# First attention of a four-block model: the eight row maxima of a batch in consecutive slots, and four steps moved with them

## The chip, the cores and the metric

The kernel runs on one core of one Trainium2 chip. The metric is the device time of one execution in microseconds, the median of several. Engine names are those of the profile: PE is the matrix engine and PEld its weight load, DVE the vector engine, ACT the scalar engine, POOL the general engine, SP the queue that issues transfers.

## The reference, cut to what matters

Four blocks follow one another on `x` of 16 batches of 256 tokens and 128 channels: a mixed attention, a feed-forward layer, a second pair of attentions and a mixture of experts. Only the first block is touched:

```
x = x + attention0(layernorm(x), ctx)
    q, cq, k, v = z @ Wq + bq, z @ Wcq + bcq, z @ Wk + bk, z @ Wv + bv     # 16 heads of 8
    ck, cv      = ctx @ Wck + bck, ctx @ Wcv + bcv                         # 64 context tokens a batch
    y  = softmax(causal(q k^T / sqrt 8)) v  +  softmax(cq ck^T / sqrt 8) cv
    out = y @ Wp + bp
```

The softmax subtracts the maximum of each row. The kernel finds the maxima of a batch with scores of its own, puts them, negated, into spare rows of the queries, and computes the scores a second time, transposed, with the maximum already taken off.

## The kernel before, in words

`l0_attention` works through 16 batches in a software pipeline. A batch has U = 10 slots; slot number s = 10 n + u is slot u of batch n, and each engine has its own program, written out slot by slot by `tensor_slot`, `vector_slot`, `scalar_slot` and `gpsimd_slot`. Each engine runs its own list strictly in order, and semaphores tie the four together. Slot u of batch n holds the second scores of one unit of that batch (u 0 to 7 self attention, u 8 and 9 context), the exponential of them on ACT, and, in between, steps of other batches. The table `SLOT` says how many slots from slot 0 of its own batch a step stands: `nm` at -3 is slot 7 of the batch before. In what follows u0 to u9 are the ten slots of the steady state, and a step is named by the u in which it falls.

The steps: `z` transposes the normalised tokens; `qk0` and `qk1` are the projections of q, cq and k of both token tiles; `v`, `ck`, `cv` those of the values and of the context; `q0`, `q1`, `k`, `kc` transpose the queries and keys; `nm` transposes the maxima; `e0`, `e1` and `e2` transpose the unnormalised outputs (self attention of both token tiles, and context), DVE divides them by their sums, and after `e2` adds the context part to the self part (`y_summed`); `e3` transposes the sum, ACT copies it out, and `e4` multiplies it with `Wp`. All of them go through a ring of two PSUM banks (6 and 7): a step on PE waits until the step two before it in the ring has been drained by DVE or ACT. Within one slot the order is that of `SLOT`: z, q0, q1, v, k, qk0, kc, ck, cv, qk1, nm, e0 to e4.

The maxima of a batch are eight steps m0 to m7: four `late` (rows 128 to 255 of the tokens), two `early`, two `cross` (context). Each is a group of matmuls into PSUM banks 2 and 3 (`tensor_max`) and a reduction over both banks by DVE (`vector_max`). Both banks are filled and read by every step, so the matmuls of m(k+1) wait for the reduction of m(k). The `late` and `early` steps come early in their slot on each engine, right behind the scores, the `cross` steps last. Before the change m0 to m4 stand in u8, u9, u0, u1 and u2, none in u3, m5 in u4, m6 in u5 and m7 in u6.

When m7 is done, `nm` puts the maxima on 32 rows, ACT copies them to `a_nmT`, SP issues four small transfers of them into the spare rows of `a_QT`, and `tensor_scores` of slot u0 waits for all four (`nm_placed`). `gpsimd_context` copies the context of a batch into `a_ctx`, for which `ck` waits. POOL also masks the exponentials (`gpsimd_select`), splits the keys (`gpsimd_stack`), raises the variances to a power (`gpsimd_rstd`) and, in u5 of batches 1 to 11, splits one piece of the feed-forward weights (`ffn.gpsimd_split`).

Slots from -40 to -1 are the lead-in: the first batches are projected and the maxima of batch 0 made before there are any scores. The slots from 164 on run inside the first slots of `l0_ffn`: slot 164 + i stands at the end of its slot i on each engine.

Of the kernel before, what the change touches and what calls it, by code (L numbers as in the profile page):

```python
# [15 lines left out]
X = mybir.AxisListType.X  # L16

P = 128
B, T, C, CC, TC = 16, 256, 128, 64, 64
# [222 lines left out]
def l0_attention(pr, mem, ffn, meanwhile):  # L242
# [4 lines left out]
    nc, io, psum = pr.nc, pr.io, pr.psum  # L247
    D, G, W = 8, 4, 32
    NM = 3 * D
    SCALE = 1.0 / float(np.sqrt(D))  # L250
    U, M, NV = 10, 8, 5
# [37 lines left out]
    nm = pr.sb("a_nm", [P, 2, 4, 2, G], F16, mem)  # L289
# [9 lines left out]
    for i in range(3):  # L299
        nc.vector.memset(V[i][:, :, :, D:D + 1], 1.0)  # L300
        for a in range(2):
# [11 lines left out]
    max_full, max_done, nm_placed = pr.sem("a_max_full"), pr.sem("a_max"), pr.sem("a_nm_placed")  # L313
# [5 lines left out]


    SLOT = {"z": -28, "q0": -20, "q1": -16, "v": -14, "k": -15, "qk0": -24, "kc": -13, "ck": -23, "cv": -13,
            "qk1": -22, "nm": -3, "e0": 12, "e1": 13, "e2": 13, "e3": 18, "e4": 20}
    MAXIMA = {m: m - (12 if m < 5 else 11) for m in range(M)}
    FIRST, LAST = -4, B + 1

    def batches(n, u, slots):

        pairs = [(part, *divmod(U * n + u - slot, U)) for part, slot in slots.items()]
        return [(part, batch) for part, batch, rest in pairs if rest == 0 and 0 <= batch < B]

    def projections(n, u):
        return batches(n, u, SLOT)
# [15 lines left out]

    first_maxima = lambda n, u: [(m, batch) for m, batch in batches(n, u, MAXIMA) if maxima[m][0] != "cross"]
    last_maxima = lambda n, u: [(m, batch) for m, batch in batches(n, u, MAXIMA) if maxima[m][0] == "cross"]  # L350

    def score_bank(n, u):

        return 2 * (u % 2) if n == B - 1 else 0


    def tensor_drained(use):
        engine, count = ring.drain[use]
        if engine == "a":
            nc.tensor.wait_ge(pro_a, count)  # L360
        else:
            nc.tensor.wait_ge(pro_v, count)
# [107 lines left out]
    def tensor_max(n, m):  # L470
        q, k, kc = QT[n % 3], KT[n % 3], KcT[n % 3]
        kind, e, pair = maxima[m]
        if m == 0:
            tensor_drained(("k", n))
        if kind == "cross":
            tensor_drained(("kc", n))
        if n or m:
            nc.tensor.wait_ge(max_done, M * n + m)
        if kind == "late":
            for x in range(2):  # L480
                for i in range(2):
                    r, g = rows(2 * e + i), 2 * pair + x
                    nc.tensor.matmul(psum[:, 2 + i, x * T:x * T + T], q[r, 0, g, P:T], k[r, g, :], start=(x == 0),
                                     stop=False, skip_group_check=True)
            for i in range(2):
                diagonal = psum[:, 2 + i, :].rearrange("p (a h k) -> p a h k", a=2, h=2)[:, :, 1, :]
                inst = nc.tensor.matmul(diagonal, pr.identb[:, :], pr.hide_later[:, 0:2, :], start=False, stop=True,  # L487
                                        skip_group_check=True)
        elif kind == "early":
            for g in range(G):  # L490
                for i in range(2):
                    r = rows(2 * e + i)
                    nc.tensor.matmul(psum[:, 2 + i, g * P:g * P + P], q[r, 0, g, 0:P], k[r, g, 0:P], start=(g == 0),
                                     stop=False, skip_group_check=True)
            for i in range(2):
                inst = nc.tensor.matmul(psum[:, 2 + i, :], pr.identb[:, :],
                                        pr.hide_later[:, :, :].rearrange("p a k -> p (a k)"), start=False, stop=True,
                                        skip_group_check=True)
        else:
            for t in range(2):  # L500
                for g in range(G):
                    for i in range(2):
                        r, to = rows(2 * e + i), (t * G + g) * TC
                        inst = nc.tensor.matmul(psum[:, 2 + i, to:to + TC], q[r, 1, g, t * P:t * P + P], kc[r, g, :],
                                                start=(t == 0 and g == 0), stop=True, skip_group_check=True)
        inst.then_inc(max_full, 1)

# [45 lines left out]
    def vector_normed(n, k):  # L553
        src = pr.x[:, 2 * n:2 * n + 2, :]
        if k == 0:
            nc.vector.wait_ge(pr.x_in[n // 2], 16)
            ln.vector_stats(n, src)
        else:
            if n >= 2:
                nc.vector.wait_ge(pro_full, ring.full(("z", n - 2)))  # L560
            ln.vector_normalise(n, z[n % 2], src).then_inc(z_ready, 1)

    def vector_max(n, m):
        kind, e, pair = maxima[m]
        pe = slice(2 * e, 2 * e + 2)
        nc.vector.wait_ge(max_full, M * n + m + 1)
        if m == 0 and n:
            nc.vector.wait_ge(pro_full, ring.full(("nm", n - 1)))
        if kind == "late":
            out, groups = nm[:, 1, pe, 0, 2 * pair:2 * pair + 2], 2  # L570
        elif kind == "early":
            out, groups = nm[:, 0, pe, 0, :], 4
        else:
            for t in range(2):
                inst = nc.vector.tensor_reduce(
                    nm[:, t, pe, 1, :], psum[:, 2:4, t * T:t * T + T].rearrange("p i (a b) -> p i a b", a=G), X,
                    ALU.max, negate=True)
            inst.then_inc(max_done, 1)
            return
        nc.vector.tensor_reduce(out, psum[:, 2:4, :].rearrange("p i (a b) -> p i a b", a=groups), X, ALU.max,  # L580
                                negate=True).then_inc(max_done, 1)

    def vector_projection(use):
# [53 lines left out]
    def vector_slot(s):  # L637
        n, u = divmod(s, U)
        for m, batch in first_maxima(n, u):
            vector_max(batch, m)  # L640
        for use in projections(n, u):
            if DRAIN[use[0]] == "v":
                vector_projection(use)
        for m, batch in last_maxima(n, u):
            vector_max(batch, m)
        for k, batch in batches(n, u, {0: -36, 1: -29}):
            vector_normed(batch, k)
        if n == B - 1 and u in (2, 5):
            ffn.vector_normed(0, u // 5)
        if n == B and u in (2, 5):  # L650
            ffn.vector_normed(1, u // 5)
# [67 lines left out]
    def gpsimd_context(n):  # L719
        if n >= 2:  # L720
            nc.gpsimd.wait_ge(pro_full, ring.full(("cv", n - 2)))
        nc.gpsimd.wait_ge(pr.ctxT_in, 16)
        nc.gpsimd.tensor_copy(ctx2[n % 2][:, :].rearrange("c (a t) -> c a t", a=2),
                              pr.ctxT[:, n:n + 1, :].to_broadcast([CC, 2, TC])).then_inc(ctx_ready, 1)
# [20 lines left out]
    def gpsimd_select(n, u):  # L745
        unit = U * n + u
        nc.gpsimd.wait_ge(exp_done, unit + 1)
        diagonal = prob[unit % 5][:, :, :].rearrange("p i (b k) -> p (i b) k", b=2)[:, :, 0:P]
        nc.gpsimd.affine_select(out=diagonal, in_=diagonal, compare_op=ALU.is_ge, fill=0.0, base=0,  # L749
                                pattern=[[0, 4], [1, P]], channel_multiplier=-1).then_inc(sel_done, 1)  # L750

    def gpsimd_slot(s):
        n, u = divmod(s, U)
        if u < 8 and 0 <= n < B:
            gpsimd_select(n, u)
        for _, batch in batches(n, u, {0: -34}):
            ln.gpsimd_rstd(batch)
        for _, batch in batches(n, u, {0: -24}):
            gpsimd_context(batch)
        for t, batch in batches(n, u, {0: -21, 1: -18, 2: -17}):  # L760
            gpsimd_stack(batch, t)
        if u == 5 and 1 <= n <= len(ffn.pieces):
            ffn.gpsimd_split(n - 1)
        if n >= B - 1 and u == 3 and n <= B:
            ffn.ln.gpsimd_rstd(n - B + 1)
# [548 lines left out]
class SelfAttention:  # L1314
# [9 lines left out]
    U, G, D = 8, 4, 32  # L1324
# [447 lines left out]
class CrossAttention:  # L1772
# [9 lines left out]
    U, G, D = 8, 4, 32  # L1782
    SLOT = {"z": -11, "k": -8, "q0": -7, "q1": -6, "v": -4, "nm": -1, "o": 14}
    SCORES, VALUES, MAXIMA = {0: 0, 1: 2}, {0: 3, 1: 5}, -4
    FIRST, LAST = -23, 8 * (B - 1) + 17
# [203 lines left out]
    def tensor_slot(self, s):  # L1989
        for e, n in self.parts(s, self.SCORES):  # L1990
            self.tensor_scores(n, e)
        for _, n in self.parts(s, {0: self.MAXIMA}):
            self.tensor_max(n)
# [73 lines left out]
    def vector_slot(self, s):  # L2067
        for _, n in self.parts(s, {0: self.MAXIMA}):
            self.vector_max(n)
# [667 lines left out]
```

## Time and profile before

| | us |
|---|---|
| median of 3 runs (1500.03 to 1508.36) | 1507.75 |
| the profiled execution's own time | 1501.43 |
| its span | 1499.7 |
| lead-in to the first scores | 0 to 48.6 |
| batches 0 to 15 of the first attention | 48.6 to about 386 |
| everything behind it | to 1499.7 |

The views used below are the page itself, the busy time of each engine in stretches of the span, the chain of work that ended last, who waited for whom, and the timeline of one engine. A timeline row has the start in us, the duration, engine and line, the operation and its operands, the count of instructions merged into it, and in square brackets the idle time before it and what ended that.

### The profile page before, as it was taken

The numbers are of one execution on the slowest core, as the hardware profiler recorded it, in microseconds if no ns is written. First come the engines' busy times: TensorE is split into PE (matmuls) and PEld (weight loads), VectorE is DVE, ScalarE is ACT, GpSimd is POOL, SyncE is SP. The second block draws the span as 40 slices with busy tenths as digits, with TensorE's granted clock in tenths as the row PEclk, the third lists the DMA queues.
The fourth block names the chain that finished last, engine by engine and source line by source line (L and its number), as shares of the span: only waits on it lengthen the run. The fifth ranks groups of instructions, "written<-read, shape, count | busy, mean of one in ns | idle before, by whom it ended". The sixth has DMA issues, their size and how long they took to land.

```text
span 1499.7 us, 42738 instructions
## 1 busy us (share of the span) xinstructions
PE 1351.0 (90%) x17848; PEld 856.9 (57%) x17848; DVE 977.7 (65%) x2238; ACT 845.7 (56%) x1309; POOL 649.5 (43%) x1118
## 2 busy tenths in 40 slices
PE   5899999997899998899999999997989999998695
PEld 2455555554344444455666666664766777677484
DVE  4777777775454544577788787745667887675232
ACT  2577777775465555657666666653456666432231
POOL 3355545543200001335666566343337775354155
PEclk9999999998999999999999999998999999998798
DMA  6000000000600000000000000012001111032351
GB/s 214 3 3 2 3 2 3 3 3 2 161 1 1 1 1 0 1 2 17 30 17 31 30 17 31 22 39 57 1 16 45 56 48 45 29 99 73 122 158 43
DMA packets 54514, 53.76 MB, mean 36 GB/s; under 512 B 9273, under 2 KB 48574, under 8 KB 54067
## 3 DMA queue, kind: packets, MB, share of 16 engines
q1 hardware_dynamic: 50482, 44.24, 9.7%
q0 software_dynamic: 2816, 6.11, 1.2%
q8 instruction: 142, 2.33, 0.7%
q10 hardware_dynamic: 1024, 0.69, 0.2%
q14 instruction: 50, 0.40, 0.1%
HBM read 20.34 MB, written 14.49 MB: 23 GB/s over the span
## 4 chain that ended last, share of the span: by engine, by line
PE 65%; DVE 12%; ACT 6%; issue 5%; POOL 5%; DMA 3%; SPq 3%; POOLq 0%; DVEq 0%; ACTq 0%
PE psum L1499 6%; PE psum L911 4%; PE psum L913 3%; PE psum L912 3%; PE psum L1182 3%; PE psum L1527 3%; DVE a_nm L580 3%; PE psum L1148 3%; PE psum L2496 2%; PE psum L2512 2%; PE psum L1976 2%; SPq L772 2%; DMA a_QT<-a_nmT 2%; DVE b_nm L1583 2%; PE psum L1985 2%
## 5 line engine op out<-in xcount | busy, mean ns | idle before, releaser
L1583 DVE TENSOR_REDUCE b_nm<-psum 128x4 f16<-128x1024 f32 x128 | 157.5, 1230 | 70.0 <-PE psum L1504 69.0
L697 ACT ACTIVATE a_prob<-psum 128x768 f32<-128x768 f32 (+1 forms) x160 | 136.1, 853 | 62.5 <-PE psum L460 60.6
L580 DVE TENSOR_REDUCE a_nm<-psum 128x4 f16<-128x1024 f32 (+1 forms) x96 | 117.4, 1223 | 50.2 <-PE psum L487 35.8
L749 POOL TENSOR_SCALAR_AFFINE_SELECT a_prob<-a_prob 128x512 f32<-128x512 f32 x128 | 81.7, 639 | 129.5 <-ACT a_prob L697 129.3
L170 POOL TENSOR_TENSOR f_ln_rstd<-f_ln_tmp,pow_half 128x4 f32<-128x4 f32 x24 | 25.3, 1056 | 204.6 <-DVE f_ln_tmp L159 204.6
L1040 ACT ACTIVATE xo_sb<-psum,f_w_h_s 128x512 f32<-128x512 f32 x64 | 44.0, 688 | 87.0 <-PE psum L913 87.0
L1499 PE MATMUL psum<-b_QTh,b_KTh 32*128 32x256 f16 x512 | 71.2, 272 | 11.7 <-DVE b_nm L1583 8.5
L1504 PE MATMUL psum<-b_KTh,b_QTh 32*128 32x256 f16 x512 | 70.7, 273 | 1.5 <-DVE b_nm L1583 1.5
L1499 PE MATMUL psum<-b_QTh,b_KTl 32*128 32x256 f16 x512 | 70.2, 268 | 0.0
L1499 PE MATMUL psum<-b_QTl,b_KTh 32*128 32x256 f16 x512 | 70.2, 267 | 0.0
L1504 PE MATMUL psum<-b_KTl,b_QTh 32*128 32x256 f16 x512 | 69.5, 268 | 0.0
L1504 PE MATMUL psum<-b_KTh,b_QTl 32*128 32x256 f16 x512 | 69.5, 268 | 0.0
L1705 POOL TENSOR_SCALAR_AFFINE_SELECT b_late<-f_hT1l 128x256 f32<-128x256 f32 x64 | 28.2, 463 | 88.7 <-ACT f_hT1l L1668 88.7
L2606 POOL DMA_INDIRECT out_dram<-m_ys,m_number x40 | 39.7, 991 | 55.2 <-DVE m_ys L2547 45.1
L980 DVE TENSOR_TENSOR f_hlastl<-xo_sb,f_hlasth 128x512 f16<-128x512 f32 x32 | 22.2, 692 | 53.0 <-ACT f_hlasth L1041 53.0
L980 DVE TENSOR_TENSOR f_hT1l<-xo_sb,f_hT1h 128x512 f16<-128x512 f32 x32 | 22.5, 702 | 51.6 <-ACT f_hT1h L1041 51.6
L911 PE MATMUL psum<-f_hT0h,f_h_wh 128*128 128x512 f16 x128 | 50.1, 392 | 5.9 <-DVE f_hT0l L974 5.9
L1499 PEld LDWEIGHTS psum<-b_QTh,b_KTh 32*128 32x128 f16 x512 | 25.4, 92 | 45.3 <-issue 27.8
L913 PE MATMUL psum<-f_hT0h,f_h_wl 128*128 128x512 f16 x128 | 50.0, 391 | 0.0
L912 PE MATMUL psum<-f_hT0l,f_h_wh 128*128 128x512 f16 x128 | 49.8, 389 | 0.0
L1511 PE MATMUL psum<-b_nmT,b_group_row 32*128 32x256 f16 x512 | 49.1, 268 | 0.0
L1668 ACT ACTIVATE f_hT0h<-psum 128x1024 f32<-128x1024 f32 x32 | 32.7, 1023 | 28.2 <-PE psum L1511 28.2
(448 smaller groups left out, 4637.8 us busy)
## 6 DMA issues: line engine op xcount, KB each, us to landing
f_h_wh<-b_rden SPq DMA_DIRECT2D x64, 128.0 KB, 2.1
f_h_wh<-c_rden SPq DMA_DIRECT2D x64, 128.0 KB, 2.1
expert_in<-empty SPq DMA_DIRECT2D x8, 662.5 KB, 11.0
m_xt<-expert_in SPq DMA_DIRECT2D x8, 662.5 KB
m_w<-in_L_ffn_w_dram SPq DMA_DIRECT2D x16, 256.0 KB
x_sb<-in_x_dram SPq DMA_DIRECT2D x8, 256.0 KB, 4.6
f_w_h_w<-in_L_ffn_h_w_dram SPq DMA_DIRECT2D x2, 1024.0 KB, 7.5
out_dram<-m_send SPq DMA_DIRECT2D x8, 256.0 KB, 2.5
```

The source lines that it names most:

```text
L580: nc.vector.tensor_reduce(out, psum[:, 2:4, :].rearrange("p i (a b) -> p i a b", a=groups), X, ALU.max, negate=True).then_inc(max_done, 1)
L697: nc.scalar.activation(prob[unit % 5][:, :, 0:width], psum[:, first:first + 2, 0:width], ACT.Exp, scale=SCALE).then_inc(exp_done, 1)
L749: nc.gpsimd.affine_select(out=diagonal, in_=diagonal, compare_op=ALU.is_ge, fill=0.0, base=0, pattern=[[0, 4], [1, P]], channel_multiplier ...
L911: nc.tensor.matmul(bank, wh[:, k, m * P:m * P + P], xh[:, k, :], start=(k == 0), stop=False)
L912: nc.tensor.matmul(bank, wh[:, k, m * P:m * P + P], xl[:, k, :], start=False, stop=False)
L913: inst = nc.tensor.matmul(bank, wl[:, k, m * P:m * P + P], xh[:, k, :], start=False, stop=(k == K4 - 1))
L1148: nc.tensor.matmul(psum[:, u % 3, :], li2[:, slot * P:slot * P + P], zT[n % 2][:, :], start=True, stop=True).then_inc(full, 1)
L1182: inst = nc.tensor.matmul(bank[:, to], hT[n % 2][:, k, to], li3[:, k, :], start=(t == 0 and k == 0), stop=True, skip_group_check=True)
L1499: t.matmul(psum[:, first_bank + i, to], key[r, g, own], q[r, g, :], start=(k + first + second == 0), stop=False, skip_group_check=True)
L1504: inst = t.matmul(psum[:, 2 + i, to], q[r, g, own], key[r, g, :], start=(k + first + second == 0), stop=(first == 1), skip_group_check=True)
L1511: inst = t.matmul(psum[:, first_bank + i, k * T:k * T + T], self.group_row[r, g, :], self.nmT[n % 2][r, :], start=False, stop=True, skip_g ...
L1583: v.tensor_reduce(self.nm[:, :, :].rearrange("p t (j r) -> p j t r", r=32)[:, 2 * e:2 * e + 2, :, g], self.pr.psum[:, 2:4, :].rearrange("p ...
```

## The change

Six edits, all in `l0_attention`:

1. m5, m6 and m7 come one slot sooner (u3, u4 and u5), so that the eight maxima stand in u8, u9, u0 to u5.
2. `nm` comes one slot sooner, in u6 behind v and qk0, in place of u7 behind kc, ck and cv. ACT's copy and SP's four transfers follow it.
3. `gpsimd_context` stands in u0, six slots sooner, in place of u6. The statistics of the layer norm go from u4 to u6, and their power on POOL from u6 to u8; the normalisation stays in u1.
4. `e2`, with its division and the sum on DVE, goes from u3 to u7 behind kc, ck and cv; `e3` goes from u8 to u9. `e4` stays in u0.
5. In batch 0 alone the odd maxima use banks 0 and 1 (free, since there are no scores yet) and the even ones 2 and 3; the matmuls of m(k) then wait for the reduction of m(k-2).
6. For batch 15, `e2` falls in slot 167 and `e3` in 169: inside slots 3 and 5 of `l0_ffn`. Before they fell in 163 and 168, the first of them still in the attention's own loop.

```diff
     SLOT = {"z": -28, "q0": -20, "q1": -16, "v": -14, "k": -15, "qk0": -24, "kc": -13, "ck": -23, "cv": -13,
-            "qk1": -22, "nm": -3, "e0": 12, "e1": 13, "e2": 13, "e3": 18, "e4": 20}
-    MAXIMA = {m: m - (12 if m < 5 else 11) for m in range(M)}
+            "qk1": -22, "nm": -4, "e0": 12, "e1": 13, "e2": 17, "e3": 19, "e4": 20}
+    MAXIMA = {m: m - 12 for m in range(M)}
...
+    def max_bank(n, m):
+
+        return 0 if n == 0 and m % 2 else 2
...
-        if n or m:
+        if n:
             nc.tensor.wait_ge(max_done, M * n + m)
+        elif m > 1:
+            nc.tensor.wait_ge(max_done, m - 1)
+        first = max_bank(n, m)
...
-                    nc.tensor.matmul(psum[:, 2 + i, x * T:x * T + T], q[r, 0, g, P:T], k[r, g, :], start=(x == 0),
+                    nc.tensor.matmul(psum[:, first + i, x * T:x * T + T], q[r, 0, g, P:T], k[r, g, :], start=(x == 0),
...
-        pe = slice(2 * e, 2 * e + 2)
+        pe, banks = slice(2 * e, 2 * e + 2), slice(max_bank(n, m), max_bank(n, m) + 2)
...
-        nc.vector.tensor_reduce(out, psum[:, 2:4, :].rearrange("p i (a b) -> p i a b", a=groups), X, ALU.max,
+        nc.vector.tensor_reduce(out, psum[:, banks, :].rearrange("p i (a b) -> p i a b", a=groups), X, ALU.max,
...
-        for k, batch in batches(n, u, {0: -36, 1: -29}):
+        for k, batch in batches(n, u, {0: -34, 1: -29}):
             vector_normed(batch, k)
...
-        for _, batch in batches(n, u, {0: -34}):
+        for _, batch in batches(n, u, {0: -32}):
             ln.gpsimd_rstd(batch)
-        for _, batch in batches(n, u, {0: -24}):
+        for _, batch in batches(n, u, {0: -30}):
             gpsimd_context(batch)
```

## Rows read from the trace of the kernel before

**Rows 1.** The page, part 1: busy time of each engine

```profile
PE 1351.0 (90%) x17848; PEld 856.9 (57%) x17848; DVE 977.7 (65%) x2238; ACT 845.7 (56%) x1309; POOL 649.5 (43%) x1118
```

**Rows 2.** Stretches: length, busy time by engine, TensorE clock, DMA share, GB/s

```profile
110.34:130.91 20.57, 18.84 (x266) 11.03 (x266) 16.18 (x34) 15.00 (x22) 11.13 (x20) 1.00 0.01 2
297.92:317.72 19.80, 18.87 (x267) 11.04 (x268) 15.40 (x29) 15.00 (x22) 8.81 (x17) 1.00 0.02 4
...
252.00:256.00 4.00, 4.00 (x37) 1.42 (x39) 2.59 (x3) 2.91 (x5) 1.05 (x2) 0.50 0.03 8
```

**Rows 3.** Chain of work that ended last, one batch: start, us, what

```profile
108.52 1.77 DMA a_QT<-a_nmT
...
111.15 1.22 DVE a_nm L580
```

**Rows 4.** Timeline of PE, one batch from u0 to u8

```profile
110.39 0.28 PE L483 MATMUL psum<-a_KT,a_QT 32*128 32x256 f16 x2
...
114.46 0.40 PE L493 MATMUL psum<-a_KT,a_QT 32*128 32x128 f16 x8
...
115.98 0.28 PE L456 MATMUL psum<-a_QT,a_KT 32*128 32x256 f16 x2
...
117.53 0.60 PE L429 MATMUL psum<-ident,a_ysT 128*128 128x128 f32 x4
...
125.51 0.68 PE L382 MATMUL psum<-a_wctx,a_ctx 64*128 64x128 f32 x4 [0.84 <-POOL a_ctx L723]
126.34 0.28 PE L409 MATMUL psum<-ident,a_nm 128*32 128x128 f16 x2 [0.15 <-DVE a_kcf L597]
126.55 0.41 PE L466 MATMUL psum<-a_QT,a_KcT 32*64 32x256 f16 x8
```

**Rows 5.** Timeline of DVE, the same batch

```profile
113.18 1.22 DVE L580 TENSOR_REDUCE a_nm<-psum 128x4 f16<-128x1024 f32 x1
...
115.43 1.23 DVE L580 TENSOR_REDUCE a_nm<-psum 128x8 f16<-128x1024 f32 x1 [0.52 <-PE psum L496]
...
118.23 0.35 DVE L624 RECIPROCAL a_denc<-psum 128x32 f32<-128x32 f32 x1
...
119.41 1.22 DVE L580 TENSOR_REDUCE a_nm<-psum 128x8 f16<-128x1024 f32 x1
...
127.65 1.23 DVE L580 TENSOR_REDUCE a_nm<-psum 128x4 f16<-128x1024 f32 x1 [0.83 <-PE psum L487]
```

**Rows 6.** Timeline of PE, a batch without a piece of weights on POOL

```profile
311.96 0.29 PE L404 MATMUL psum<-ident,a_kctok 64*128 64x64 f16 x4
...
312.72 0.49 PE L382 MATMUL psum<-a_wctx,a_ctx 64*128 64x128 f32 x2 [0.17 <-ACT a_KcT L668]
313.13 0.29 PE L409 MATMUL psum<-ident,a_nm 128*32 128x128 f16 x2
```

**Rows 7.** Timeline of PE, the lead-in

```profile
28.64 0.61 PE L483 MATMUL psum<-a_KT,a_QT 32*128 32x256 f16 x4 [1.32 <-DVE a_nm L580]
...
43.87 0.29 PE L409 MATMUL psum<-ident,a_nm 128*32 128x128 f16 x2 [0.52 <-DVE a_kcf L597]
...
48.65 0.28 PE L456 MATMUL psum<-a_QT,a_KT 32*128 32x256 f16 x2 [1.81 <-DMA a_QT<-a_nmT]
```

**Rows 8.** Timeline of PE: m4 of batch 15, then its first slot

```profile
341.33 0.40 PE L493 MATMUL psum<-a_KT,a_QT 32*128 32x128 f16 x8 [0.54 <-DVE a_nm L580]
...
355.86 0.40 PE L456 MATMUL psum<-a_QT,a_KT 32*128 32x256 f16 x2 [0.52 <-DMA a_QT<-a_nmT]
```

**Rows 9.** Timeline of PE and ACT, the end of the attention inside the feed-forward

```profile
385.75 1.19 PE L438 MATMUL psum<-a_wp,a_yT 128*128 128x128 f32 x4 [4.54 <-ACT a_yT L675]
...
386.21 0.63 ACT L1033 ACTIVATE f_hT0h<-xo_sb 128x512 f16<-128x512 f32 x1 [0.60 <-DVE xo_sb L969]
```

**Rows 10.** Chain of work that ended last: a reduction in u0 of two batches

```profile
235.08 1.23 DVE a_nm L580
...
278.15 1.23 DVE a_nm L580
```

More of the change, by code:

```diff
@@ L482, in tensor_max @@
                     r, g = rows(2 * e + i), 2 * pair + x
-                    nc.tensor.matmul(psum[:, 2 + i, x * T:x * T + T], q[r, 0, g, P:T], k[r, g, :], start=(x == 0),
+                    nc.tensor.matmul(psum[:, first + i, x * T:x * T + T], q[r, 0, g, P:T], k[r, g, :], start=(x == 0),
                                      stop=False, skip_group_check=True)
             for i in range(2):
-                diagonal = psum[:, 2 + i, :].rearrange("p (a h k) -> p a h k", a=2, h=2)[:, :, 1, :]
+                diagonal = psum[:, first + i, :].rearrange("p (a h k) -> p a h k", a=2, h=2)[:, :, 1, :]
                 inst = nc.tensor.matmul(diagonal, pr.identb[:, :], pr.hide_later[:, 0:2, :], start=False, stop=True,
@@ L492, in tensor_max @@
                     r = rows(2 * e + i)
-                    nc.tensor.matmul(psum[:, 2 + i, g * P:g * P + P], q[r, 0, g, 0:P], k[r, g, 0:P], start=(g == 0),
+                    nc.tensor.matmul(psum[:, first + i, g * P:g * P + P], q[r, 0, g, 0:P], k[r, g, 0:P], start=(g == 0),
                                      stop=False, skip_group_check=True)
             for i in range(2):
-                inst = nc.tensor.matmul(psum[:, 2 + i, :], pr.identb[:, :],
+                inst = nc.tensor.matmul(psum[:, first + i, :], pr.identb[:, :],
                                         pr.hide_later[:, :, :].rearrange("p a k -> p (a k)"), start=False, stop=True,
@@ L503, in tensor_max @@
                         r, to = rows(2 * e + i), (t * G + g) * TC
-                        inst = nc.tensor.matmul(psum[:, 2 + i, to:to + TC], q[r, 1, g, t * P:t * P + P], kc[r, g, :],
+                        inst = nc.tensor.matmul(psum[:, first + i, to:to + TC], q[r, 1, g, t * P:t * P + P], kc[r, g, :],
                                                 start=(t == 0 and g == 0), stop=True, skip_group_check=True)
@@ L575, in vector_max @@
                 inst = nc.vector.tensor_reduce(
-                    nm[:, t, pe, 1, :], psum[:, 2:4, t * T:t * T + T].rearrange("p i (a b) -> p i a b", a=G), X,
+                    nm[:, t, pe, 1, :], psum[:, banks, t * T:t * T + T].rearrange("p i (a b) -> p i a b", a=G), X,
                     ALU.max, negate=True)
```

## The prediction

> **What bounds the kernel now.** I read the page first: PE is busy 90% and DVE 65% [rows 1], but these are averages over four blocks, and only the first attention, 338 of 1500 us, is touched. So I cut that stage by batch. A batch of the steady state takes 20.57 us, of which PE is busy 18.84 and DVE 16.18 [rows 2]: PE is nearest to the bound and still idles 1.7 us. Batches 1 to 11 of this kind carry a piece of weights on POOL; the next batch takes 19.80 us [rows 2].
>
> The idle time of PE in a batch is of three kinds. First, ck stands 0.84 us because POOL's copy of the context is late, and nm another 0.15 behind DVE's drain of ck [rows 4]. In the batch without a piece of weights that wait is gone; only cv waits 0.17 us for ACT's copy of kc [rows 6]. Second, u0 waits for the transfer of the maxima; it lands at 110.29 (108.52 + 1.77, rows 3), and m2's matmuls start at 110.39 [rows 4]. Third, the maxima wait for one another. A reduction takes 1.22 us, 0.05 later PE may refill the banks, and a late step is ready for DVE 0.76 later (m2: PE at 110.39, DVE at 111.15, rows 3 and 4). So late steps follow one another at 2.03 us: 111.15, 113.18 [rows 3, 5]. The early m4 needs 0.97 on PE (114.46, rows 4; 115.43, rows 5), so its distance is 2.25.
>
> The reader should see that two of these bind at once in u0: m1's reduction ends 0.05 before 110.39 too (one step of 2.03 before m2's start of reduction, plus its 1.22: 111.15 - 2.03 + 1.22 = 110.34). Taking away the transfer's wait frees only the two scores matmuls ahead of m2, which overlap m2 anyway.
>
> **The change part by part.** I walk one batch of the changed kernel from m4's matmuls at 114.46 [rows 4], with u8 to u2 as before, since their maxima already go hand over hand.
>
> *m5 in u3.* m4's reduction ends at 115.43 + 1.23 = 116.66 [rows 5]; m5 starts at 116.71. PE has done u3's scores by 116.25 (115.98 + 0.27) and stands 0.46 us. This wait is new; behind it in PE's order are the values and e1, and ACT gets its next scores later. In u4 before, m5 found its banks free. PE then does m5 0.76, the values 0.79, e1 0.49, u4's scores 0.27 and q1 0.54 (distances between starts on PE's timeline): m6 starts at 119.56, past m5's reduction (116.71 + 0.97 + 1.23 = 118.91). PE sets the pace again from here.
>
> *m6, m7, nm.* m6 0.28, u5's scores 0.27 with 0.14 of waiting for ACT, the values 0.79, k 0.55: m7 at 121.59. Then m7 0.28, u6's scores 0.27, v 0.65, qk0 0.85, 0.07 for DVE's drain of v (queued behind m7's reduction), nm 0.22: u7 at 123.93. nm starts at 123.71 in place of 126.34 [rows 4], so its transfers land 2.6 us sooner, long before u0. On SP nothing else is queued.
>
> *kc, ck, cv, e2 in u7.* Scores 0.27, values 0.79, kc; the context has been there since u0. But cv still waits for ACT's copy of kc: it starts 0.76 behind kc (311.96 to 312.72, rows 6) and takes 0.41. Before, this wait lay under the late context. Then e2, 0.53 (it started at 117.53, rows 4, and u4's scores at 118.06), moved here from u3. Sum: u8 at 123.93 + 1.06 + 0.76 + 0.41 + 0.53 = 126.69, against 126.55 [rows 4]. What the context's wait gave (0.99), the new wait in u3 (0.46), the uncovered copy of kc and the two cross steps, less well overlapped, have taken back.
>
> *The sum on DVE.* e2's matmuls now end just ahead of u8. They are done 0.60 behind their start at 126.16, and DVE needs 1.18 from the first reciprocal until m's reduction may start (118.23 to 119.41, rows 5): 126.16 + 0.60 + 0.05 + 1.18 = 127.99. m0's matmuls would be ready at 127.79. So m0's reduction starts at 127.99 against 127.65 before [rows 5], and everything to the next m4 is the chain of reductions, which hands the delay on: +0.34, say +0.3 us for each of the 11 batches with a piece, +3.3.
>
> The batch without a piece was shorter by 20.57 - 19.80 = 0.77 us [rows 2]; with the changed order the piece makes no difference any more, so there the change costs 0.34 + 0.77 = +1.1 for each of two batches: +2.2.
>
> Bounds for a batch: from -1.5 (both named waits go, 0.48 + 0.99, and nothing comes in their place) to +1.1 (what the walk gives with no late context to win back). I take +0.3, as each term is a distance in this trace.
>
> *Statistics, power and context moved.* DVE's statistics (0.9 us) go behind qk0's drain in u6, where PE's next need of DVE is kc 1 us later; POOL has no mask to make in u8. Cost nothing under these covers; without them at most their own 0.9 us, and then only against the copy of ck.
>
> *e3 in u9, e4 in u0.* ACT's queue in u9 is an exponential, a copy and a cast, then e3's copy; e4 wants it 1.3 us into u0. ACT had 0.40 us idle there. Nothing, at most 0.4.
>
> *Batch 0.* In the lead-in PE stands 1.32 us before m2 [rows 7], as much before m4, 0.47 before m3 and 0.89 before m5. With two bank pairs these go, and m5 to m7 come sooner by a slot. I walked it with the low clock's durations: m2 27.1, m3 29.0, m4 29.9, m5 32.6 (z waits for the normalisation that DVE queues behind m3), m6 34.8, m7 36.4, nm 39.5 in place of 43.87 [rows 7]. Batch 1's m0 then starts about 41.3 instead of 44.09, and m2 in u0, at the end of the chain of two reductions, 3.2 us sooner than with the first scores at 48.65 [rows 7]. So nm's 4.4 us don't arrive whole, because batch 1's own maxima bind next. -3.2, between 0 and -5.
>
> *Batch 15.* In batch 14 no projections are left and the maxima bind alone. From m4 at 341.33 [rows 8] the chain gives m5 343.58, m6 345.9, m7 347.7, nm 349.6, and 4.6 us later (nm at 313.13, rows 6, to the next u0 at 317.72, rows 2) u0 at 354.3 in place of 355.86 [rows 8]: -1.5. In its tail the feed-forward's PE stands 4.54 us for ACT's copy of e3 [rows 9]. One slot later that copy is queued behind the cast at 386.21 as well [rows 9] (before, it started at 385.23), some 1.6 us; e2's DVE work out of the way of the first product gives back some 0.7. +0.9.
>
> **Sum:** -3.2 + 3.3 + 2.2 - 1.5 + 0.9 = +1.7 us. Against the profiled execution's own 1501.43 that is 1503; against the median of 1507.75 it would be 1509. The shown runs lie at 1500 and at 1508, so neither is a firm base; I say 1507.
>
> **The clock.** Over a whole batch the granted clock is 1.00 in spite of the small waits [rows 2]. The Trainium skill (TensorE: Matmul & The Clock Gate, section on psum-queue depth-cycling) tells of a kernel whose PE idles briefly between groups while it cycles through PSUM banks and whose clock goes up and down because of it. No steady batch but one does so here; the rival below is what it would mean.
>
> **The rivals.**
>
> *The waits simply go.* If m5 didn't stand in u3 and DVE weren't late for m0, each batch would lose its 1.47 us: -16.2 for eleven, -1.3 for two, with the ends (-3.8) -21 us: 1486. For it: PE is the busiest engine, and both waits are on the chain. Against it: the chain of reductions, tied with the transfer in u0. Chance 0.10.
>
> *Clock dips.* The slower side. Once, at 252 to 256, the clock fell to half, 0.50 [rows 2], some 3 us behind the wait for the context in a thin stretch of PE's work. The two batches around it took 278.15 - 235.08 = 43.07 us [rows 10] in place of 41.14: 1.9 us a dip. The change spreads PE's idling over u9 to u3, where m1 to m5 all stand. If that made each of 14 batches dip once, it would cost 27 us more: 1534. It decides from eight dips on (15 us). The profile's clock of 1.00 speaks against, and the stretch after kc gets denser. Chance 0.05.
>
> *The slot edit doesn't overlap anything in batch 0* (PE was the limit there): +3.2 on the sum, 1510, inside my case. Chance 0.15. The forecast, a loss of a few tenths in each batch balanced by the lead-in, has the other 0.70.
>
> **How the numbers follow.** A measurement of this kernel tells about 1%, 15 us, from no change. Forecast and third rival lie within it, save for 0.01 below and 0.02 above, where the walk errs by 1 us a batch. Faster over 1% 0.11, within 0.82, slower 0.07. The range takes the per-batch term from -0.9 to +0.9 less the ends, and the 8 us between the runs: 1491 to 1517.
>
> **What would show it.** Right: m5's matmuls start in u3 behind an idle of about 0.46 put down to DVE; ck no longer waits for POOL, cv waits for ACT; m0's reduction starts right behind DVE's sum; u0 has no wait for the transfer, but the batch still takes 20.6 to 21.1 us; the first scores start near 45; e4 of batch 15 stands longer. Wrong: a batch of 19 to 20 us, or several batches with a clock of about 0.8. The walk would be wrong if PE's steps overlap otherwise than in their present order, since each tenth in a batch is 1.4 us in all.

## The result and the profile after

The changed kernel takes 1514.84 us (median of 20 runs, 1505.62 to 1520.43) against 1505.09 for the kernel before (median of 20). The ratio is 1.0056, 95% interval 1.0041 to 1.0071: 8.4 us slower (the two medians are 9.75 apart). The forecast was 1507 with a loss of 1.7 us inside the noise; the loss is clear of it.

A batch first. The stretches below run from u8's scores to the next u8's; columns are length, busy time of PE, PEld, DVE, ACT and POOL, the granted clock, the DMA share and GB/s. After the change:

```profile
44.68:64.44 19.76, 17.34 (x189) 8.34 (x188) 11.20 (x19) 10.31 (x15) 7.80 (x15) 0.68 0.01 2
106.65:127.88 21.23, 19.89 (x267) 10.96 (x266) 16.35 (x36) 14.89 (x22) 11.13 (x21) 1.00 0.01 2
```

The second line answers to the 20.57 us of [rows 2]: 0.66 us more in ten of the batches 1 to 11 (batch 1 took 20.98), at the same clock of 1.00. The first is batch 0 from its first scores to u8, and its clock is 0.68.

The timeline of PE after the change, from u8 to the next u8:

```profile
107.54 0.81 PE L382 MATMUL psum<-a_wcat,a_zT 128*128 128x384 f32 x2
...
109.26 0.39 PE L490 MATMUL psum<-a_KT,a_QT 32*128 32x256 f16 x4 [0.57 <-DVE a_nm L587]
...
115.37 0.40 PE L500 MATMUL psum<-a_KT,a_QT 32*128 32x128 f16 x8
...
117.62 0.40 PE L500 MATMUL psum<-a_KT,a_QT 32*128 32x128 f16 x8 [0.40 <-DVE a_nm L587]
117.95 0.60 PE L503 MATMUL psum<-hide_later,identb 128*128 128x512 bf16 x2
118.49 0.64 PE L527 MATMUL psum<-a_prob,a_V 128*32 128x256 f32 x8
...
119.28 0.66 PE L426 MATMUL psum<-ident,a_ysT 128*128 128x128 f32 x4
119.86 0.28 PE L460 MATMUL psum<-a_QT,a_KT 32*128 32x256 f16 x2
...
124.84 0.28 PE L413 MATMUL psum<-ident,a_nm 128*32 128x128 f16 x2
...
126.88 0.48 PE L386 MATMUL psum<-a_wctx,a_ctx 64*128 64x128 f32 x2 [0.17 <-ACT a_KcT L675]
127.30 0.66 PE L433 MATMUL psum<-ident,a_ysT 128*128 128x128 f32 x4
127.88 0.41 PE L470 MATMUL psum<-a_QT,a_KcT 32*64 32x256 f16 x8
```

Read it against [rows 4]. The wait of ck for POOL is gone and that of u0 for the transfer too. In their place m5 (117.62) stands 0.40 us for m4's reduction, cv 0.17 for ACT's copy of kc, and m1 (109.26) 0.57 for m0's reduction. The last comes of DVE, whose timeline has the sum of e2 right ahead of m0's reduction:

```profile
106.80 0.36 DVE L631 RECIPROCAL a_denc<-psum 128x32 f32<-128x32 f32 x1
107.19 0.42 DVE L633 TENSOR_TENSOR a_yc<-psum,a_denc 128x256 f32<-128x256 f32 x1
107.65 0.42 DVE L636 TENSOR_TENSOR a_y<-a_y,a_yc 128x256 f32<-128x256 f32 x1
107.99 1.22 DVE L587 TENSOR_REDUCE a_nm<-psum 128x4 f16<-128x1024 f32 x1
```

u8's scores started at 106.65, so m0's reduction comes 1.34 us behind them; before it was 127.65 - 126.55 = 1.10 [rows 4, 5]. So both halves of the batch are longer: from m4's matmuls to u8 it is 12.51 us (115.37 to 127.88) against 12.09 (114.46 to 126.55, rows 4), and from u8 to the next m4 0.24 more, which is DVE's sum.

Where the 8 us lie by the two traces, from one u8 to the next: u8 of batch 0 is 0.4 us sooner (64.44 against 64.84); batches 1 to 11 take 21.23 us each against 20.57, in all 4.6 us more, since the trace of before had three longer batches (22.50, 20.91, 20.74) in them; batches 12 to 15 take 1.45, 1.55, 0.98 and 0.10 us more. u8 of batch 15 starts at 375.21 against 366.98: +8.2 us. From there to the first matmul of the feed-forward's second layer it is 22.29 us against 21.04, and at the first reduction of the second attention the changed kernel is 8.0 us late (634.5 against 626.5). The two profiled executions differ by more, 1513.0 against 1499.7 us of span: the other 5.3 us arise behind 990 us, in code that the change leaves alone, and the execution profiled before was 3.7 us faster than its kernel's median. What follows therefore counts the traces up to the end of the first attention only.

### The profile page after: what moved, and what is told of

Read it like the earlier page. It is cut to its first block, busy times and chain, and to the rows that moved or that the text cites. A ratio compares the mean times of both kernels' runs of the same rounds, so it can differ in the third digit from the quotient of the medians.

```text
span 1513.0 us, 42738 instructions
## 1 busy us (share of the span) xinstructions
PE 1368.8 (90%) x17848; PEld 858.4 (57%) x17848; DVE 979.1 (65%) x2238; ACT 844.7 (56%) x1309; POOL 651.2 (43%) x1118
## 3 DMA queue, kind: packets, MB, share of 16 engines
HBM read 20.34 MB, written 14.49 MB: 23 GB/s over the span
## 4 chain that ended last, share of the span: by engine, by line
PE 70%; DVE 15%; ACT 6%; issue 4%; POOL 2%; DMA 1%; SPq 1%; POOLq 0%; DVEq 0%; ACTq 0%
PE psum L1506 6%; DVE a_nm L587 5%; PE psum L918 4%; PE psum L919 3%; PE psum L1189 3%; PE psum L920 3%; PE psum L1534 3%; PE psum L1155 3%; PE psum L2503 2%; PE psum L527 2%; PE psum L2519 2%; PE psum L1983 2%; DVE b_nm L1590 2%; PE psum L1992 2%; PE psum L1930 2%
## 5 line engine op out<-in xcount | busy, mean ns | idle before, releaser
L582 DVE TENSOR_REDUCE a_nm<-psum 128x8 f16<-128x512 f32 x64 | 41.2, 686 | 20.8 <-PE psum L511 20.8
```

## The experiments

Twelve kernels ran. In the diffs, only the lines that differ from the kernel named are shown. "A batch" is the distance from u8 to u8 that most of the batches 1 to 11 of one profile share to 0.02 us. Single batches are longer in several kernels, and each kernel has one profile only.

### Each edit alone, on the kernel before

**The third edit** (context, statistics, power):

```diff
-        for k, batch in batches(n, u, {0: -36, 1: -29}):
+        for k, batch in batches(n, u, {0: -34, 1: -29}):
...
-        for _, batch in batches(n, u, {0: -34}):
+        for _, batch in batches(n, u, {0: -32}):
             ln.gpsimd_rstd(batch)
-        for _, batch in batches(n, u, {0: -24}):
+        for _, batch in batches(n, u, {0: -30}):
             gpsimd_context(batch)
```

> The kernel before with the third edit alone: the context copied in u0, statistics in u6, power in u8. Theory (each batch is a chain of PE and DVE steps, and the late context is a real link of it): batches 1 to 11 go from 20.57 us to the 19.80 us of the batch that had no piece of weights, ck no longer waits for POOL, the kernel is 8 us faster (ratio 0.995). Rival (the context's wait is covered by the transfer of the maxima in u0, as both reach u0 together): a batch stays at 20.5 us and the time is unchanged.

Measured: ratio 1.0004 (0.9977 to 1.0032), a batch 20.40 us (two of 20.76 and 20.74). Neither theory: the context's wait is gone, but nm stands. What the batches give, the ends of its trace take back: u8 of batch 0 comes at 68.73 against 64.84, and batches 14 and 15 take 4.2 us more; why wasn't tried.

```profile
129.05 0.49 PE L382 MATMUL psum<-a_wctx,a_ctx 64*128 64x128 f32 x2 [0.17 <-ACT a_KcT L668]
130.08 0.28 PE L409 MATMUL psum<-ident,a_nm 128*32 128x128 f16 x2 [0.54 <-DVE a_kcf L597]
```

Its DVE shows why; the statistics moved to u6 run between m7's reduction and the drain of ck, for which nm waits:

```profile
127.67 1.28 DVE L575 TENSOR_REDUCE a_nm<-psum 128x8 f16<-128x512 f32 x2
128.87 0.47 DVE L150 BATCH_NORM_STATS2 aln_stat<-x_sb 128x6 f32<-128x128 f32 x2
129.38 0.25 DVE L154 BATCH_NORM_AGGREGATE aln_mv<-aln_stat 128x2 f32<-128x6 f32 x2
129.66 0.17 DVE L159 TENSOR_SCALAR aln_tmp<-aln_mv 128x2 f32<-128x2 f32 x1
129.74 0.28 DVE L597 TENSOR_TENSOR a_kcf<-psum,a_bctx 64x128 f32<-64x128 f32 x1
```

**The fourth edit** (sums): `"e2": 13, "e3": 18` becomes `"e2": 17, "e3": 19`.

> The kernel before with the fourth edit alone: e2 and its sum in u7, e3 in u9. Theory (DVE's 1.2 us of division and sum now stand ahead of m0's reduction, which heads the chain m0 to m4): m0's reduction starts right behind the sum and a batch takes 20.9 to 21.1 us, the kernel is 4 to 7 us slower. Rival (the sums are harmless, the loss is all in the maxima): a batch of 20.6 us, within 1 us of before.

Measured: ratio 1.0114 (1.0076 to 1.0153), 17 us where the theory had 4 to 7, a batch 21.23 us, and five of the eleven 23.1 to 23.4. So this edit alone costs as much per batch as the whole change, and PE's clock falls in batches besides:

```profile
104.73:125.97 21.24, 19.32 (x267) 11.01 (x267) 16.19 (x34) 14.98 (x22) 11.09 (x20) 1.00 0.01 2
170.51:193.92 23.41, 22.02 (x267) 11.64 (x266) 16.42 (x34) 15.09 (x22) 11.08 (x20) 0.85 0.01 3
```

Two batches of one kernel with the same instructions; the second has a clock of 0.85 and is 2.2 us longer. This is the mechanism of my slower rival, in a kernel that the rival didn't name; the changed kernel's profile has no such batch between 1 and 11.

**The first two edits** (maxima and nm): `"nm": -3` becomes `-4`, `m - (12 if m < 5 else 11)` becomes `m - 12`.

> The kernel before with the first two edits alone: m5, m6, m7 and nm one slot sooner. Theory (m5's matmuls now stand in u3 behind m4's reduction, and everything on PE behind them is late): an idle of 0.4 us before m5, u0 waits no longer for the transfer, a batch takes 21.0 to 21.3 us, the kernel is 5 to 9 us slower. Rival (the transfer's wait of 0.48 us was a real link): a batch of 20.1 to 20.3 us, 4 us faster.

Measured: ratio 1.0057 (1.0037 to 1.0076), a batch 20.96 us; PE idles 0.40 us before m5, and u0 shows no wait for the transfer. The theory holds (its batch was 0.04 too long), the rival falls: without its wait in u0 a batch is longer, not shorter. These edits also cost time ahead of the steady batches: u8 of batch 0 comes at 69.70 against 64.84.

**The fifth edit** (two bank pairs in batch 0): the lines with `max_bank` of the diff above.

> The kernel before with the fifth edit alone: the odd maxima of batch 0 on banks 0 and 1. Theory (the lead-in gets shorter, but PE's clock stays at half for longer, so that batch 0 gives it back): nm of batch 0 some 3 us sooner, the first scores 2 to 4 us sooner, u8 of batch 0 less than 1 us sooner, the kernel's time the same within 1.5 us. Rival (the lead-in's gain arrives whole, and the other edits ate it): u8 of batch 0 is 3 us sooner and the kernel 3 us faster.

Measured: ratio 0.9969 (0.9948 to 0.9990). The first scores come at 45.12 against 48.65 [rows 7], u8 of batch 0 at 62.93 against 64.84: half of the 3.5 us is given back in batch 0, between theory and rival. The expected "same" falls, if narrowly: the ratio says 1.5 to 7.8 us, 4.7 by its middle, of which the trace shows 1.9 in batch 0 (the profiled execution was the slowest of the twelve, 1508.54 us).

### From the fastest kernel back to the changed one

**The context's copy alone**, statistics and power left where they were:

```diff
-        for _, batch in batches(n, u, {0: -24}):
+        for _, batch in batches(n, u, {0: -30}):
             gpsimd_context(batch)
```

> The kernel before with the context's copy alone moved to u0; statistics and power stay in u4 and u6. Theory (in the run with the whole third edit it was DVE's statistics, now ahead of its drain of ck, that nm waited 0.54 us for, not the context any more): nm waits for nothing but kc's copy, batches 1 to 11 take 19.8 us, the kernel is 7 to 9 us faster (ratio 0.995). Rival (something else reaches u7 just after the context, such as POOL's masks behind the piece of weights): 20.4 us a batch as in that run, 0 to 2 us faster.

Measured: ratio 0.9905 (0.9888 to 0.9923), a batch 19.79 us. On the timeline of PE only u0 (108.58) and cv (123.37) still stand:

```profile
108.58 0.28 PE L456 MATMUL psum<-a_QT,a_KT 32*128 32x256 f16 x2 [0.49 <-DMA a_QT<-a_nmT]
...
123.37 0.48 PE L382 MATMUL psum<-a_wctx,a_ctx 64*128 64x128 f32 x2 [0.17 <-ACT a_KcT L668]
```

Eleven batches at 0.78 us are 8.6 us; the measured 14 us are more. Three of before's batches were longer than 20.57 in its profile and one of this kernel's was longer than 19.79 (20.34), so that u8 of batch 15 comes 11.1 us sooner by the traces (355.86 against 366.98); the rest of the difference isn't found in the first attention.

**The same with two bank pairs in batch 0.**

> The kernel before with the context's copy alone moved, and the two bank pairs in batch 0. Theory (the two parts touch different stretches and add up): 11 to 13 us faster than before (ratio 0.992), u8 of batch 0 some 2 us sooner, then 19.8 us a batch. Rival (with less waiting the clock falls more often, so that the sum does not arrive): under 8 us faster.

Measured: ratio 0.9885 (0.9870 to 0.9900), 1491.57 us, the lowest median, and 17 us where the theory had 11 to 13. The bank pairs' own part, 0.9885 against 0.9905, isn't clear of the noise: the intervals overlap. u8 of batch 0 comes at 60.88 against 64.62 with the context's copy alone: here all 3.8 us of the lead-in arrive. The two stretches from the first scores to u8, with the two bank pairs alone, and with the context's copy too:

```profile
45.12:62.93 17.81, 16.26 (x186) 8.43 (x187) 10.31 (x20) 10.00 (x13) 8.50 (x16) 0.71 0.01 2
```

```profile
44.70:60.88 16.18, 14.26 (x185) 7.76 (x186) 10.26 (x19) 9.89 (x13) 8.52 (x16) 0.79 0.01 3
```

Equal work, clocks of 0.71 and 0.79, 1.6 us apart: by these two, what of the lead-in's gain arrives is a matter of where PE's clock comes back.

**m5 alone into u3**, with the context's copy in u0: `m - (12 if m < 5 else 11)` becomes `m - (12 if m < 6 else 11)`.

> The kernel before with the context's copy in u0 (as in the run that gave 19.79 us a batch), and m5 alone moved from u4 to u3; m6, m7 and nm stay. Theory (m5's matmuls find their banks held by m4's reduction and PE stands with all of u3 and u4 queued behind): an idle of 0.40 us before m5 in each batch, u5 starts 5.8 us behind m4's matmuls in place of 5.1, a batch takes 20.4 to 20.6 us, 8 us more than without this edit. Rival (the wait in u3 is won back in u4, where PE has less to do): 19.8 to 20.0 us.

Measured: ratio 1.0034 (1.0009 to 1.0059), a batch 20.88 us, 1.09 more than without the edit, and more than the theory's 0.7; the kernel is 1.3%, 19 us, slower than without it, where the theory had 8. First PE here, from m4 to u5, then ACT, then PE of the kernel before in u4:

```profile
137.16 0.40 PE L493 MATMUL psum<-a_KT,a_QT 32*128 32x128 f16 x8
...
139.41 0.40 PE L493 MATMUL psum<-a_KT,a_QT 32*128 32x128 f16 x8 [0.39 <-DVE a_nm L580]
...
140.28 0.64 PE L520 MATMUL psum<-a_prob,a_V 128*32 128x256 f32 x8
...
142.09 0.28 PE L456 MATMUL psum<-a_QT,a_KT 32*128 32x256 f16 x2
...
142.40 0.62 PE L393 MATMUL psum<-ident,a_tok 128*128 128x128 f16 x8
143.33 0.28 PE L456 MATMUL psum<-a_QT,a_KT 32*128 32x256 f16 x2 [0.31 <-ACT a_prob L697]
```

```profile
142.47 0.81 ACT L697 ACTIVATE a_prob<-psum 128x768 f32<-128x768 f32 x1 [2.60 <-PE psum L460]
```

```profile
118.06 0.28 PE L456 MATMUL psum<-a_QT,a_KT 32*128 32x256 f16 x2
...
118.24 0.38 PE L493 MATMUL psum<-a_KT,a_QT 32*128 32x128 f16 x8
...
119.00 0.61 PE L393 MATMUL psum<-ident,a_tok 128*128 128x128 f16 x8
```

From m4 to u5 it is 6.17 us here against 5.08 in the kernel before (114.46 to 119.54). By distances between starts the 1.09 has three parts. m5 starts 0.46 us later than PE was free for it (0.39 of it shown as idle). u5's scores (143.33) wait for ACT's exponential of u4, which isn't queued late, since ACT had been idle 2.60 us when u4's scores came; PE, with m5 gone from u4, reaches u5 before it is done, and that costs 0.39. And m5 takes 0.87 us in u3 (139.41 to 140.28), while u4 gets shorter without it by 0.63 only (from the scores to the next transposes 0.94 with it, 0.31 without): in u4 it began 0.18 us behind the scores and ran into them. That is the last 0.24.

**All of m5, m6, m7 and nm**, with the context's copy in u0.

> The kernel before with the context's copy in u0, and m5, m6, m7 and nm one slot sooner. Theory (the first two edits alone make the batch of the run that had all but the sums): 20.8 us a batch in place of 19.79, no wait for the transfer in u0, 12 us more than without them, of which m5 is two thirds. Rival (statistics on DVE in u6 or the two bank pairs had a share in that run's 20.83): 20.4 us or less.

Measured: ratio 1.0080 (1.0050 to 1.0110), a batch 20.96 us. m6, m7 and nm add 0.08 to m5's 1.09. Not two thirds but nearly all of it is m5. The whole kernel is 26 us slower than without these edits, where the theory had 12: eleven batches at 1.17 are 12.9, and u8 of batch 0 comes at 70.74 against 64.62. On the kernel before the same two edits cost 0.39 a batch (20.57 to 20.96), not 1.17: there the wait of ck for the context shrank in exchange, from 0.84 to 0.28 us.

**The sums alone**, with the context's copy in u0: `"e2": 17, "e3": 19`.

> The kernel before with the context's copy in u0, and e2 with its sum in u7, e3 in u9. Theory (0.14 us of PE, as transposes overlap less well there, and 0.24 us of DVE ahead of m0): a batch takes 20.1 to 20.3 us in place of 19.79, 4 to 6 us more than without it. Rival (what made this edit alone cost 0.66 us a batch was the late context): 19.8 to 19.9 us.

Measured: ratio 1.0030 (1.0006 to 1.0053), a batch 20.67 us, 0.88 more, and 19 us in all where the theory had 4 to 6. My 0.4 was too small, for a reason that the profile names:

```profile
126.00 0.66 PE L429 MATMUL psum<-ident,a_ysT 128*128 128x128 f32 x4 [0.47 <-DVE a_Vc L607]
126.59 0.41 PE L466 MATMUL psum<-a_QT,a_KcT 32*64 32x256 f16 x8
...
129.16 0.39 PE L483 MATMUL psum<-a_KT,a_QT 32*128 32x256 f16 x4 [0.53 <-DVE a_nm L580]
```

With nm still in u7, e2 is two behind cv in the ring of banks and waits 0.47 us for DVE to drain cv. In the changed kernel nm is in u6, e2 is two behind ck, and that wait doesn't exist: the two edits are coupled through the ring.

**The changed kernel with the sums moved back**: `"e2": 13, "e3": 18`.

> The changed kernel with e2 and its sum back in u3 and e3 back in u8; maxima, nm, context, statistics and banks stay moved. Theory (e2 in u7 costs 0.58 us of PE behind the context and 0.24 us of DVE ahead of m0): m0's reduction starts 1.1 us behind u8 in place of 1.34, a batch takes 20.7 to 20.9 us in place of 21.23, the kernel is 4 to 6 us faster than the changed one (ratio to before 1.002). Rival (the wait of m5 in u3 is the whole loss, e2's place is neutral): 21.1 to 21.3 us a batch, ratio 1.0055.

Measured: ratio 0.9997 (0.9980 to 1.0014), a batch 20.83 us in place of 21.23. The theory holds in the batch: the sums cost 0.40 us each in the changed kernel. The kernel is 9 us faster than the changed one, where the theory had 4 to 6.

**The changed kernel with DVE's order turned**: division and sum of e2 behind m0's reduction, PE untouched.

```diff
+        for use in batches(n, u, {"e2": 18}):
+            vector_projection(use)
         for use in projections(n, u):
-            if DRAIN[use[0]] == "v":
+            if DRAIN[use[0]] == "v" and use[0] != "e2":
```

> The changed kernel with one edit: DVE does e2's division and sum behind m0's reduction, not ahead of it; PE's order is untouched. Theory (0.24 us of the 0.66 a batch is DVE standing in the way of m0's reduction): m0's reduction starts 1.1 us behind u8, a batch takes 21.0 us in place of 21.23, the kernel is 2 to 4 us faster than the changed one (ratio to before 1.0035). Rival (e3 in u9 now waits for the sum, or qk1's drain comes too late for q0): still 21.2 us or more.

Measured: ratio 1.0078 (1.0061 to 1.0095), a batch 21.73 us, the longest of all (in the whole time only the fourth edit alone is slower). m0's reduction does come 1.10 us behind u8 (107.16, 108.26), but the next one is late:

```profile
108.26 1.23 DVE L587 TENSOR_REDUCE a_nm<-psum 128x4 f16<-128x1024 f32 x1 [0.98 <-PE psum L494]
109.40 0.35 DVE L631 RECIPROCAL a_denc<-psum 128x32 f32<-128x32 f32 x1
109.78 0.42 DVE L633 TENSOR_TENSOR a_yc<-psum,a_denc 128x256 f32<-128x256 f32 x1
110.24 0.42 DVE L636 TENSOR_TENSOR a_y<-a_y,a_yc 128x256 f32<-128x256 f32 x1
110.58 0.55 DVE L599 TENSOR_TENSOR a_qf<-psum,a_bcat 128x384 f32<-128x384 f32 x1
111.05 1.22 DVE L587 TENSOR_REDUCE a_nm<-psum 128x4 f16<-128x1024 f32 x1
```

m0 to m1 is 2.79 us in place of 2.03: between two reductions DVE has 0.8 us to spare while PE refills the banks, and the sum with qk1's drain is 1.65. The rival's number (21.2 or more) came true, but neither of its causes was this one; the step ahead of m0 was the cheaper place for the sum, as PE had work of its own there.

**kc in u6**, on the fastest version: `"kc": -13` becomes `-14`.

> The fastest kernel so far (the context's copy in u0, two bank pairs in batch 0) with one more edit: kc from u7 to u6, so that ACT's copy of it is over when cv wants its bank. Theory: cv waits no longer for ACT (0.17 us idle, 0.35 with what the weight load waits), a batch takes 19.4 to 19.6 us, the kernel is 3 to 5 us faster than without it (ratio to before 0.986). Rival (the chain of the maxima or the transfer of u0 takes over): 19.7 us or more.

Measured: ratio 0.9908 (0.9881 to 0.9935), a batch 19.78 us as without it. The rival holds: the whole kernel isn't faster either. cv no longer waits, and u0's wait for the transfer grows from 0.49 to 0.90 us:

```profile
145.32 0.28 PE L460 MATMUL psum<-a_QT,a_KT 32*128 32x256 f16 x2 [0.90 <-DMA a_QT<-a_nmT]
```

The chain of that kernel goes from m7's reduction to the drain of ck, nm, ACT's copy, three issues on SP of 0.64 us, the transfer, and m2 in u0. cv isn't in it. This is the transfer's wait as a real link, which it becomes once everything ahead of it is early.

### The batch, term by term

| kernel | a batch, us | step |
|---|---|---|
| before | 20.57 | |
| context's copy in u0 | 19.79 | -0.78 |
| and m5 in u3 | 20.88 | +1.09 |
| and m6, m7, nm sooner | 20.96 | +0.08 |
| and statistics, power, two bank pairs | 20.83 | -0.13 |
| and the sums in u7 and u9: the changed kernel | 21.23 | +0.40 |

Every line is a run. The steps hold in this order only: the first two edits cost 0.39 on the kernel before and 1.17 behind the context's copy, and the sums 0.66, 0.88 or 0.40, by what stands around them. The statistics' place costs where nm stands behind ck (20.40 against 19.79) and helps a little where nm is in u6: on the fourth line nm waits 0.15 us for DVE's drain of v, on the fifth it doesn't. Statistics and power weren't run apart there; the bank pairs touch batch 0 alone.

## Why the prediction was wrong

Inside the steady batch its mechanism was right and its sizes too small: a batch became longer by the wait of m5 and DVE's sum, and the context's gain was spent on them. At both ends a step itself was wrong. The forecast was +1.7 us, the measured difference 8.4. By the two traces, up to the feed-forward's second layer, it is +9.5, and the terms are: batch 0 -0.4 (forecast -3.2), batches 1 to 11 +4.6 (+3.3), batches 12 and 13 +3.0 (+2.2), batches 14 and 15 +1.1 (-1.5), the tail +1.25 (+0.9). The +4.6 looks nearer to the forecast than it is: it has 2.4 us of longer batches in the profile of before taken off, which is luck; by the batch that recurs the eleven cost 7.3.

*The batch of the steady state, "say +0.3 us for each of the 11 batches".* Measured 0.66. The walk from m4 to u8 gave 12.23 us; it is 115.37 to 127.88 = 12.51. The step that failed is "the distances between starts on PE's timeline": I took m5 as 0.76, e1 as 0.49 and e2 as 0.53, the distances that they had in the old order. In the new order m5 takes 0.87 (117.62 to 118.49), e1 0.58 (119.28 to 119.86), e2 0.58 (127.30 to 127.88). These are 0.25 of the 0.28; with 0.04 more from u8 to m0's reduction and 0.04 lost in rounding, that is the difference, and it puts the batch over the 21.1 that I had given as the sign of being right. Times eleven it is 4 us.

*The context, -0.8 a batch.* Right: 19.79 where I had read 19.80 off the batch without a piece of weights. I costed it inside the sum and not as an edit by itself, which hid that it alone was worth 1%.

*m5 in u3.* The wait was forecast at 0.46 and is that (116.89 + 0.27 to 117.62; the profile shows 0.40 of it as idle). Its full price is 1.09 where m5 alone is moved, since the time that it shared with u4's scores goes, and u4 becomes too short for ACT's exponential.

*e2 ahead of m0.* Forecast 1.30 us from u8 to the reduction, measured 1.34.

*Statistics, "cost nothing under these covers".* Right in the changed kernel, wrong by itself: "only against the copy of ck" was the very thing, 0.54 us for nm in the kernel with the third edit alone.

*Batches without a piece, +1.1.* Measured 1.45 and 1.55, by the same terms.

*Batch 0, -3.2.* The lead-in's walk was right: nm came 5.0 us sooner (38.83 against 43.87; forecast 39.5) and the first scores 4.0 (44.68, "near 45"), but u8 only 0.4. The step that failed is that I carried the gain through batch 0 as if its clock were that of before; the stretch was at 0.68 against 0.79. The first scores of the changed kernel and of the one with the context's copy and the bank pairs alone come at the same time:

```profile
44.68 0.39 PE L460 MATMUL psum<-a_QT,a_KT 32*128 32x256 f16 x2
```

```profile
44.70 0.28 PE L460 MATMUL psum<-a_QT,a_KT 32*128 32x256 f16 x2 [1.81 <-DMA a_QT<-a_nmT]
```

In the first PE is at half clock already, and full clock comes back at about 57.2 us, as late as in the kernel before (57.3); in the second it starts at full clock, falls, and is back at about 53.3, and the gain arrives whole. The two kernels with the first two edits and without the bank pairs reach u8 of batch 0 some 5 to 6 us later than without these edits, so that the sooner maxima may be what keeps the clock down; one profile of each doesn't show it, and the kernel with the fourth edit alone, the same as before up to that point, is there 2.4 us sooner than before (62.46 against 64.84). Why the clock comes back sooner in one than in another stays open. The result is near that of my third rival (no gain from the lead-in), for another reason.

*Batch 15, -1.5.* Wrong in sign: from m4 of batch 15 to its first slot it is 15.83 us (348.19 to 364.02) against 14.53 before, +1.3, and batches 14 and 15 together took 1.1 us more. nm now stands in u6 and waits for m7's reduction, with u7's scores behind it on PE:

```profile
355.33 0.22 PE L464 MATMUL psum<-a_QT,a_KT 32*128 32x128 f16 x2
356.87 0.27 PE L413 MATMUL psum<-ident,a_nm 128*32 128x128 f16 x2 [1.31 <-DVE a_nm L582]
357.07 0.28 PE L460 MATMUL psum<-a_QT,a_KT 32*128 32x256 f16 x2
```

The step that failed is "4.6 us later" from nm to the next u0. I took that distance from a batch in which nm is the last step of u7, so that only u8 and u9 lie in it; behind an nm in u6 lies u7 too, and it is 7.15 us (356.87 to 364.02), part of it at half clock. I had named what m5 holds up in its queue, and not what nm does.

*The tail, +0.9.* Measured +1.25, by another path. "e4 of batch 15 stands longer" didn't come: it stands 0.54 us in place of 4.54. PE stands 3.50 us before e3 instead (its transposes start at 393.63), for DVE's sum, which is queued behind the feed-forward's own work on DVE. That the size is near is luck.

*The rivals.* "The waits simply go" is refuted by the run with the context's copy and the maxima, which shows neither ck's wait for POOL nor u0's for the transfer and has a batch of 20.96 us against 20.57 all the same. The clock dips, at 0.05, are not in this kernel's steady batches but cost the kernel with the fourth edit some 10 us (five batches of 2 us). The changed kernel's runs tend to be slower where the mean clock is lower: 1505.6 us at a mean of 0.968, 1520.4 at 0.955.

## What to carry to other kernels

When an order is moved, a step's time isn't the distance it had before, but that with its new neighbour, and a distance taken from the old order holds only if the same steps lie in it: check on each moved matmul group what it ran alongside, and put a tenth of a microsecond of doubt on each, times the number of rounds. In a chain where two engines hand one buffer back and forth, a slot without such a step is not a gap to be closed: it is where the other engine's extra work and PE's backlog fit. Cost each edit of a bundle by itself, and on the kernel that it will stand in, as one may be worth more than the whole: here one line, the context's copy, is worth 1%, and the rest took away 1.5%.

## What the runs showed of the hardware that was not expected

What a group of matmuls costs depends on what it begins beside. The eight small matmuls of m5 and their mask lengthen u4 by 0.63 us, where they begin 0.18 us behind the scores, and u3 by 0.87, where the scores are over. That the difference is time shared on PE is read from the starts; it wasn't tried apart. And the granted clock falls in single batches of one kernel (five of eleven at about 23.2 us, 0.85) and in none of the eleven of another whose batch is as long (21.23 us, 1.00 throughout), though PE is busy for 19.32 us in a 21.24 us batch of the first and 19.89 in 21.23 of the other.
